# Causal attention of 16 heads: scores from three-part bf16 stacks of one head, or from two-part f32r stacks with two heads in the two halves of the array

## The reference

```python
x = x + 0.5 * ffn(layernorm(x))            # x: 4 x 1024 x 256, top-2 of 8 experts
x = x + attn(layernorm(x))
x = x + 0.5 * ffn(layernorm(x))

def attn(x):                                # 16 heads of 16
    Q = (x @ W_dq) @ W_uq                   # latents of 64
    c_kv = x @ W_dkv
    K, V = c_kv @ W_uk, c_kv @ W_uv
    scores = einsum('bqhd,bkhd->bhqk', Q, K) / 4
    scores = where(causal, scores, -inf)
    out = einsum('bhqk,bkhd->bqhd', softmax(scores), V)
    return out @ W_o
```

## Time and profile before

| | us |
|---|---|
| median of three runs | 1443.84 |
| span of the profiled execution | 1440.9 |
| the two undisturbed runs, beside that span | 1443.74 and 1443.84 |
| projections | 373 to 473 |
| first row maxima | 473 to 513 |
| attention loop | 513 to 1024.6 |

### The profile page before, as it was taken

How to read it: one execution, slowest core, us unless ns; L and a number is a source line. 1 busy time by engine, 2 the same in 40 slices (tenths; PEclk the granted TensorE clock), 3 DMA queues, 4 the chain that set the end, 5 groups by cost and what they waited for, 6 DMA issues and landing times. The chain is left out here.

```text
span 1440.9 us, 28115 instructions
## 1 busy us (share of the span) xinstructions
PE 1111.1 (77%) x7114; PEld 671.0 (47%) x7117; DVE 853.0 (59%) x2530; ACT 674.2 (47%) x1676; POOL 463.3 (32%) x520
## 2 busy tenths in 40 slices
PE   3458988875786589999899899998694698897840
PEld 2246766664332134444334334443372577676630
DVE  5763333332884688888788788884177533333335
ACT  3513343332455056766666666666454243333320
POOL 3636666653234400000000000000165456665620
PEclk8558999998778589999999999999897599999975
DMA  7502222223586914555544444440273022222238
GB/s 244 182 1 81 82 79 80 83 77 103 179 262 173 167 16 61 78 74 78 73 60 60 61 60 61 72 57 9 84 232 110 19 75 84 80 81 75 76 122 264
DMA packets 130285, 141.06 MB, mean 98 GB/s; under 512 B 46800, under 2 KB 104592, under 8 KB 130192
## 3 DMA queue, kind: packets, MB, share of 16 engines
q1 hardware_dynamic: 116368, 102.24, 31.8%
q0 software_dynamic: 13824, 37.77, 8.3%
HBM read 86.88 MB, written 52.69 MB: 97 GB/s over the span
## 5 line engine op out<-in xcount | busy, mean ns | idle before, releaser
L1407 ACT ACTIVATE t_prob<-t_psS 128x512 f32<-128x512 f32 (+3 forms) x768 | 328.1, 494 | 189.1 <-PE t_psS L1339 155.6
L1427 DVE CUSTOM_DVE_ANT_0 t_psR<-t_psR,all_causal 128x128 f32<-128x128 f32 (+3 forms) x512 | 246.4, 505 | 60.4 <-PE t_psR L1317 52.9
L1317 PE MATMUL t_psR<-stacks_kst,stacks_qst 96*128 96x512 bf16 (+3 forms) x768 | 231.2, 345 | 29.3 <-PEq L886 20.3
L1336 PE MATMUL t_psS<-stacks_qst,stacks_kst 99*128 99x512 bf16 (+3 forms) x768 | 224.0, 329 | 2.7 <-ACT t_prob L1407 2.0
L1431 DVE TENSOR_REDUCE t_maxp<-t_psR 128x1 f32<-128x512 f32 x256 | 176.0, 688 | 21.1 <-PE t_psR L1317 20.3
L1350 PE MATMUL t_psO<-t_prob,t_vst 128*32 128x512 f32 (+3 forms) x1536 | 163.6, 498 | 3.0 <-ACT t_prob L1407 1.1
L1317 PEld LDWEIGHTS t_psR<-stacks_kst,stacks_qst 96*128 96x128 bf16 x768 | 70.1, 98 | 201.0 <-DVE t_maxp L1427 103.1
L1308 POOL COPY t_vst<-stacks_v_rows 128x512 f32<-128x512 f32 x16 | 9.9, 616 | 443.3 <-DMA stacks_v_rows<-v_rows 443.2
L670 PE MATMUL be_psG<-b_w,be_xT 128*128 x432 | 119.8, 413 | 13.0 <-issue 8.6
L670 PE MATMUL ae_psG<-a_w,ae_xT 128*128 x432 | 118.2, 408 | 14.3 <-issue 8.1
L763 DVE TENSOR_TENSOR ae_hid<-ae_sg,ae_psG 128x256 f32<-128x256 f32 x72 | 30.4, 422 | 139.1 <-ACT ae_sg L733 106.8
(11 more groups left out here) (284 smaller groups left out, 1901.1 us busy)
## 6 DMA issues: line engine op xcount, KB each, us to landing
qk_parts<-q_parts SPq DMA_DIRECT2D x32, 384.0 KB, 2.8
stacks_qst<-qk_parts SPq DMA_DIRECT2D x96, 128.0 KB, 4.7
stacks_kst<-qk_parts SPq DMA_DIRECT2D x96, 128.0 KB, 7.4
q_yk<-y_rows SPq DMA_DIRECT2D x16, 512.0 KB, 5.4
s_yk<-y_rows SPq DMA_DIRECT2D x16, 512.0 KB, 5.4
o_rows<-t_orow SPq DMA_DIRECT2D x32, 136.0 KB, 8.8
bl_raw<-o_rows SPq DMA_DIRECT2D x8, 544.0 KB, 4.0
xn_rows<-al_xn SPq DMA_DIRECT2D x8, 512.0 KB, 4.3
```

What stands on the lines that cost most here:

```text
L1317: nc.tensor.matmul(psR[bank][:, 0:w], qst[slot][0:KROWS, h, i * P:(i + 1) * P], kst[slot][0:KROWS, h, k0:k0 + w], start=True, stop=True).t ...
L1336: ins = nc.tensor.matmul(ps, kst[k][0:MROWS, h, j * P:(j + 1) * P], qst[k][0:MROWS, h, a:(c + 1) * 512], start=True, stop=a > j * P)
L1407: nc.scalar.activation(prob[j % 2][:, h, a:(c + 1) * 512], psS[n % ST_BANKS][:, a - c * 512:512], ACT.Exp, scale=DK ** -0.5).then_inc(exp_ ...
L1427: ins = nc.vector.tensor_tensor_reduce(psR[bank][:, 0:w], psR[bank][:, 0:w], T.causal[:, 512 - w:512], 1.0, -BIG, ALU.add, ALU.max, maxp[: ...
```

## The change

- Q and K are split in two f32r parts, high and the rest; middle and low parts, and the steps that made them, are gone. `qst` takes parts 0,0,1 and `kst` 0,1,0: 48 rows for a head, 50 with the two rows of the maximum. Head h lies in rows 0 to 49 or 64 to 113 (`rows(h % 2, ...)`), so a pair of heads fills both halves of the array. Twelve loads remain, of two heads each.
- V stays on chip (`A.values`), and GpSimd spreads it into `vst` from there; its way through DRAM is gone. GpSimd fills the constant rows during the projections.
- Row scores come as units of one pair (blocks 2 to 7) or two pairs (blocks 0 and 1) over two PSUM banks, 22 in a group, in a ring of two slots. The causal mask is added to them by TensorE, and VectorE reduces both heads in one instruction.
- Transposed scores go through query half 0 first, then half 1, with three `prob` buffers and one output bank. The output of a group is turned, copied and stored as one piece.
- The plan has new costs; an output is turned at the sixth place of the ring. In the projections VectorE writes the second part straight from PSUM; of the constant fills, the first load of a stack waits for all.

```diff
-PARTS = 3
-Q_PARTS = (0, 0, 0, 1, 1, 2)
-K_PARTS = (0, 1, 2, 0, 1, 0)
+PARTS = 2
+Q_PARTS = (0, 0, 1)
+K_PARTS = (0, 1, 0)
 KROWS = len(Q_PARTS) * DK
 MROWS = KROWS + PARTS
+HALVES = 2
+HPAIRS = HG // HALVES
+HROWS = P // HALVES
 VW = 32
 OW = DK + 1
 SLOTS = 3
-RING_BANKS = 3
+RING_SLOTS = 2
+RING_W = 1024
 ST_BANKS = 3
-AHEAD = 11
-READER_LATENCY = 1000
+PROBS = 3
+AHEAD = 5
+OUT_AT = 5
+READER_LATENCY = 200
...
+    N_LOADS = HALVES * (len(Q_PARTS) + len(K_PARTS))
+
+    def __init__(self, M, qk_dram):
+        self.qk_dram = qk_dram
+        self.values = M.sb("values", [P, NT, D])
+        self.qst = [M.sb(f"qst{s}", [P, HPAIRS, S], F32R) for s in range(SLOTS)]
+        self.kst = [M.sb(f"kst{s}", [P, HPAIRS, S], F32R) for s in range(SLOTS)]
+        self.vst = [M.sb(f"vst{s}", [P, QT, HG * VW]) for s in range(SLOTS)]
         self.loaded = [M.sem(f"loaded{s}") for s in range(SLOTS)]
+        self.fixed_ready = M.sem("fixed_ready")
+
+    def heads(self, rows, width):
+        return rows[:].rearrange("p j (h w) -> p (j h) w", w=width)
+
+    def fixed(self, nc, pool):
+
+        c = Chain(pool, self.fixed_ready)
+        for s in range(SLOTS):
+            c.link(nc.gpsimd.memset(self.kst[s][:].bitcast(F32), 1.0))
+            c.link(nc.gpsimd.memset(self.vst[s][:], 0.0))
+            c.link(nc.gpsimd.memset(self.heads(self.vst[s], VW)[:, :, DK:DK + 1], 1.0))
+
+    N_FIXED = 3 * SLOTS
...
+                by_half = src.rearrange("(hp a d) t -> a d hp t", a=HALVES, d=DK)
+                for half in range(HALVES):
+                    row = half * HROWS + r * DK
+                    sp.dma_start(st[slot][row:row + DK, :, :].bitcast(F32), by_half[half]).then_inc(self.loaded[slot], 16)
...
-                for u in range(NU if now else 0):
-                    hold(pool, mid_ready, c * NU + u + 1, T)
-                    nc.gpsimd.tensor_tensor(parts[:, u, 2, :], left[:, u % 2, :], parts[:, u, 1, :],
-                                            ALU.subtract).then_inc(low_ready, 1)
-            steps(pool, step)
+            A.fixed(nc, pool)
...
-            def middle(c, u):
-                act.wait_ge(left_ready, c * NU + u + 1)
-                nc.scalar.copy(parts[:, u, 1, :], left[:, u % 2, :]).then_inc(mid_ready, 1)
...
     units = []
-    for h in range(HG):
-        for i in range(QT):
-            end = (i + 1) * P
-            units.append((h, i, 0, min(end, 512), i))
-            if end > 512:
-                units.append((h, i, 512, end - 512, i + QT // 2))
+    for i in range(QT):
+        if i < 2:
+            units.append((i, 0, HPAIRS, 256, 0, (i + 1) * P))
+        else:
+            for k0 in range(0, (i + 1) * P, 512):
+                units += [(i, hp, 1, 512, k0, min((i + 1) * P - k0, 512)) for hp in range(HPAIRS)]
     return units
 
 
+def score_steps():
+
+    return [(j, c, max(j * P - c * 512, 0)) for c in range(2) for j in range(QT) if j * P < (c + 1) * 512]
...
+        psR = [M.ps(f"psR{i}", [P, RING_W]) for i in range(RING_SLOTS)]
         psS = [M.ps(f"psS{i}", [P, 512]) for i in range(ST_BANKS)]
-        psO = [M.ps(f"psO{i}", [P, 512]) for i in range(2)]
-        o_stored = [M.sem(f"o_stored{c}") for c in range(2)]
-        m_loaded, filled, drained, max_ready, m_ready, st_done, exp_done, pv_done, o_copied, pool_done, chain = (
+        psO = M.ps("psO", [P, 512])
...
+                for half in range(HALVES):
+                    for part in range(PARTS):
+                        row = half * HROWS + KROWS + part
+                        sp.dma_start(qst[slot][row:row + 1, :, :].bitcast(F32),
+                                     mparts[half * (HPAIRS * QT):(half + 1) * (HPAIRS * QT), part, :].bitcast(F32)).then_inc(m_loaded, 16)
...
+            def rows(half, n):
+                return slice(half * HROWS, half * HROWS + n)
+
+            def score(u, stack, r, slot):
+
+                i, hp0, pairs, pitch, k0, w = units[u]
+                ps = psR[slot]
+                wait(pe, drained, r + 1 - RING_SLOTS)
+                diagonal = k0 + w == (i + 1) * P
+                for hp in range(pairs):
+                    for half in range(HALVES):
+                        at = half * 512 + hp * pitch
+                        ins = nc.tensor.matmul(ps[:, at:at + w], qst[stack][rows(half, KROWS), hp0 + hp, i * P:(i + 1) * P],
+                                               kst[stack][rows(half, KROWS), hp0 + hp, k0:k0 + w],
+                                               start=hp == 0, stop=not diagonal and hp == pairs - 1)
+                if diagonal:
+                    for half in range(HALVES):
+                        blocks = ps[:, half * 512:half * 512 + pairs * pitch].rearrange("p (n w) -> p n w", w=pitch)
+                        ins = nc.tensor.matmul(blocks[:, :, w - P:w], T.ident_bf[:], bc(T.causal[:], 1, [P, pairs, P]),
+                                               start=False, stop=True)
+                ins.then_inc(filled, 1)
...
+            def score_t(g, k, n, h):
+                s, (j, c, a) = n * HG + h, sequence[n]
+                ps = psS[s % ST_BANKS][:, a:512]
+                diagonal = c * 512 <= j * P
+                wait(pe, exp_done, g * ST + s + 1 - ST_BANKS)
+                ins = nc.tensor.matmul(ps, kst[k][rows(h % HALVES, MROWS), h // HALVES, j * P:(j + 1) * P],
+                                       qst[k][rows(h % HALVES, MROWS), h // HALVES, c * 512 + a:(c + 1) * 512],
+                                       start=True, stop=not diagonal)
+                if diagonal:
                     ins = nc.tensor.matmul(ps[:, 0:P], T.ident_bf[:], T.causal_t[:], start=False, stop=True)
                 ins.then_inc(st_done, 1)
...
+                for n, (j, c, a) in enumerate(sequence):
+
+                    wait(act, pv_done, g * PV + n + 1 - PROBS)
                     for h in range(HG):
-                        n, a = n_st[j, c, h], max(c * 512, j * P)
-                        act.wait_ge(st_done, g * ST + n + 1)
-                        nc.scalar.activation(prob[j % 2][:, h, a:(c + 1) * 512], psS[n % ST_BANKS][:, a - c * 512:512], ACT.Exp,
+                        s = n * HG + h
+                        act.wait_ge(st_done, g * ST + s + 1)
+                        nc.scalar.activation(prob[n % PROBS][:, h, a:512], psS[s % ST_BANKS][:, a:512], ACT.Exp,
                                              scale=DK ** -0.5).then_inc(exp_done, 1)
-                    if j == QHALF + 1:
+                    if n == 0 and with_before:
+                        copy_out(g - 1, 1)
+                    if n == last_of[0] + 1:
+                        if with_before:
+                            act.wait_ge(drained, out_at(g - 1))
                         copy_out(g, 0)
-                copy_out(g, 1)
 
             steps(step)(act)
+            copy_out(NG - 1, 1)
...
+            def row_max(u, r, slot):
+
+                i, hp0, pairs, pitch, k0, w = units[u]
+                out = maxq[:, :, hp0:hp0 + pairs, i] if i < QHALF else maxp[:, k0 // 512, :, hp0:hp0 + pairs, i - QHALF]
+                dve.wait_ge(filled, r + 1)
+                scores = psR[slot][:].rearrange("p (a n w) -> p a n w", a=HALVES, w=pitch)[:, :, 0:pairs, 0:w]
+                nc.vector.tensor_reduce(out, scores, AX_X, ALU.max).then_inc(drained, 1)
+
+            def join_max(r):
 
                 dve.wait_ge(drained, r)
-                link(nc.vector.tensor_copy(maxq[:, :, 0:QHALF], maxp[:, :, 0:QHALF]), g, 1)
-                nc.vector.tensor_tensor(maxq[:, :, QHALF:QT], maxp[:, :, QHALF:QT], maxp[:, :, QT:QT + QHALF],
-                                        ALU.max).then_inc(max_ready, 1)
-
-            def split_max(g, r, bank):
-
+                nc.vector.tensor_tensor(maxq[:, :, :, QHALF:QT], maxp[:, 0], maxp[:, 1], ALU.max).then_inc(max_ready, 1)
+
+            def split_max(g, r, slot):
+
+                ps = psR[slot][0:MROW, 0:P]
                 dve.wait_ge(filled, r + 1)
-                wait(dve, m_loaded, g * (16 * PARTS))
-                nc.vector.tensor_scalar(neg[:], psR[bank][0:MROW, 0:P], -1.0, None, ALU.mult).then_inc(drained, 1)
-                dve.wait_ge(drained, r + 1)
-                link(nc.vector.tensor_copy(mparts[:, 0], neg[:]), g, 2)
-                link(nc.vector.tensor_tensor(mid[:], neg[:], mparts[:, 0], ALU.subtract), g, 3)
-                link(nc.vector.tensor_copy(mparts[:, 1], mid[:]), g, 4)
-                nc.vector.tensor_tensor(mparts[:, 2], mid[:], mparts[:, 1], ALU.subtract).then_inc(m_ready, 1)
-
-            def copy_rows(g, c, r, bank):
+                wait(dve, m_loaded, g * (16 * N_MAX))
+                link(nc.vector.tensor_scalar(mparts[:, 0], ps, -1.0, None, ALU.mult), g)
+                nc.vector.scalar_tensor_tensor(mparts[:, 1], ps, -1.0, mparts[:, 0], ALU.mult, ALU.subtract).then_inc(m_ready, 1)
+                dve.wait_ge(m_ready, g + 1)
+                nc.vector.sem_inc(drained, 1)
```

(14 more changed lines are left out.)

317 lines of the change are left out of this document (133 added, 184 removed).

## The result

The changed kernel takes 1891.47 us (median of 4 runs, 1887.9 to 1901.85), the kernel before 1446.3 us (median of 4, 1443.74 to 1455.33): ratio 1.309, 95% interval 1.305 to 1.314. Slower, as forecast, but 236 us more than the 1655 us, and 91 us above the top of the range.

What follows compares the result with a forecast made beforehand. TensorE was taken as the bound. 1440.9 us + 157 (TensorE's queue) + 62 (clock) - 8 (projections) = 1652, and about 3 us from span to run gave 1655 us; range 1490 to 1800.

Steps and rivals of the forecast that it cites:

- The clock: In the attention loop: two groups' worth of half clock, +62 us, between ends of 0 and 146.
- Rival 3: In the attention loop: the clock stays at half throughout, +434 us, 2089 us in all; chance 0.05.
- Changes of tiling and loads in the open: TensorE per loop group: 107 changes instead of 24, 10.0 us, and weight loads at 49 entries into 64 rows, 5.1 us.
- The whole queue at full clock: TensorE per loop group: 38.9 us of streams, changes and loads, plus 3.2 us of waits left as they are.
- the term of +157 us: TensorE's queue in the attention loop: 38.9 us a group against 29.1, +9.8, times 16 groups.
- A group at half: One loop group wholly at half clock: 31 us more than at full clock, 73 us.
- Halves overlap: Row scores of two heads stream at once in the array's two halves: 4.0 us a group instead of 7.9.
- rival 4: Score matmuls of two heads don't overlap in the halves: +4.0 + 0.9 us per group, +78, 1733 us; chance 0.04.
- 128-column f32r in four passes: Bound on TensorE's loop queue: these matmuls take four passes as f32 values do, +1.9 us per group, +31 us.
- VectorE and ScalarE: In the loop: 22.4 and 21.7 us per group, under TensorE's 38.9, so they add nothing.
- Projections: Projections stage: a shorter chain saves 1 us per chunk, -8 us (0 to -20).
- Rival 1: Diagonal steps: changes cost nothing and TensorE gains what it no longer streams, 27.0 us per group, 1351 us; chance 0.11.

Runs made afterwards that it cites:

- the run with 48 rows: Kernel before, score matmuls on their first 48 rows only, causal masks left out, exponential's factor 10,000 times smaller: 1751.19 us, ratio 1.216.
- run 4: Changed kernel, score matmuls over the rows of both halves (full height), masks added as two matmuls of 64 rows: 1750.03 us, ratio 1.217.
- run 9: Changed kernel, transposed scores read 64 rows in place of 50, the added ones zeros against ones: 1813.81, 1835.1, 1850.72 and 1851.95 us, ratio 1.283.
- 11: Changed kernel, masks added in the halves (two matmuls of 64 rows) and transposed scores on all 64 rows of their half: 1475.01 us, ratio 1.026.
- run 3: Changed kernel, score matmuls over the rows of both halves (full height), masks as they are: 1532.9 us, ratio 1.066.
- run 1: Changed kernel, each causal mask added from its score's own half as two matmuls of 64 rows: 1522.36, 1600.32, 1625.9 and 1635.4 us.
- run 2: Changed kernel, all causal masks of row scores and transposed scores left out: 1464.8 us, ratio 1.011.

## Why the prediction was wrong, step by step

- **The clock** is the step that failed. I put it at two groups' worth of half clock, +62 us. The projections' share carried over gave 146 as its upper end, and I took less than half of it because the clock there falls behind waits "which the loop lacks". Measured: 82% of the loop at half clock. From 39 to 42 us a group to 60.6 is 19 to 22, times 16 some 300 to 350 us for a term of 62. The reason given was weak in itself: the loop before has two waits of 2.0 us (up to 707.08 and 806.89), and its clock falls in the first. And in the changed loop no wait is needed for a fall. I looked for what would idle the engine and took the share of streaming time (0.57) as the warning; I named "a third of that on half of the rows" but gave it no price. The run with 48 rows shows that this, with 2 more changes of tiling a group than before, holds the clock at 0.50. What held it down, by the runs: first the scores on half of the rows (0.59 to 0.86 with as many changes, from the changed kernel to run 4), then the full-height masks between them (0.65 to 0.92 from run 9 to 11). The forecast's own sign was right: a mean clock of the loop under 0.75 makes the term far too small. Rival 3, at 0.05, had the mechanism's outcome, though not its whole extent (1.00 of the loop for 0.82) nor its cause.
- **Changes of tiling and loads in the open**, 15.1 us a group: right in place, 0.47 us for a forecast of 0.46, and 8.0 us a group for 84 changes between runs 3 and 4. 6 to 9 come back between the changed kernel and run 1, which pays for 60 more small matmuls. The sum left out loads in the open where the tiling stays (run 3), and the times that it gave for runs 1, 2 and 3 at full clock are 3 to 6 us a group short (in runs 1 and 2 waits for ScalarE are in that). A slip without weight: 107 x (0.14 - 0.093) for the changes at half clock is 5.0, not 4.3.
- **The whole queue at full clock**, 42.1 us with its waits: 39 to 42 by the two estimates above, which makes the term of +157 us 107 to 155. In part this is luck: of the 3.2 us of waits kept in it TensorE has 1.2 left (18.2 us in 15 groups), and the loads left out make up for them. **A group at half**: 73, estimated 67 to 69.
- **Halves overlap**: yes. The two of 512 columns at 707.82 are over in 0.50 us, and the next start comes after 0.34 (708.16), where two of full height took 0.42 or more. So rival 4 falls. The Trainium skill ("TensorEngine Tiling (Array Packing)", Theoretical Speedup) gives up to 2x for such a contraction. The overlap is there, but the loop with 48 rows shows the other side: at half clock, two at once are no faster than two in turn at full clock (845.52 to 845.95, 0.43 us for two of 512 columns).
- **128-column f32r in four passes**: no. A score of 128 columns with its mask takes 0.41 us (708.37 to 708.78), one of 256 takes 0.47: less, by one stream of 128 columns.
- **VectorE and ScalarE** cost nothing: right, both wait for TensorE. **Projections** -8: the first transpose of the maxima comes 8.2 us earlier; values on chip alone make the kernel before 4.6 us shorter.
- **Rival 1** falls for a second reason: even with no mask a group at full clock is 30.9 us, not 27.0, since TensorE then waits for ScalarE in turn (run 2), which a sum of TensorE's streams can't see.

## What to carry to other kernels

Packing two short contractions into the halves of the array saves time only if the granted clock holds: before such a change, run the kernel before with its matmuls cut to the rows that they would have, and read the clock. Keep every matmul between them (masks, small additions) in the same tiling, and fill the rows of a tile with zeros where they are free. Price a TensorE plan at both levels of the clock and give the level a chance of its own. When a plan changes bf16 operands for f32r, price the longer load behind every short matmul, and not only behind a change of tiling.
